# A decoder of four layers on one core: another PSUM bank and another order in the last steps of the self-attentions, and in the third cross-attention queries and rows through the bank of the outputs

## The reference

```python
def _layernorm(x, axis=-1, eps=1e-05):
    m = jnp.mean(x, axis=axis, keepdims=True)
    v = jnp.var(x, axis=axis, keepdims=True)
    return (x - m) / jnp.sqrt(v + eps)
...
    x = _layernorm(x + _L3_attn_ref(x, L3_attn_w_qkv, ...), axis=-1)
    x = _layernorm(x + _L3_xattn_ref(x, ctx_768, ...), axis=-1)
```

```python
        Qp = query @ Wq + bq
        K = _l2norm(key @ Wk + bk)
        V = value @ Wv + bv
        Q = _l2norm(Qp)
        ...
        out = out @ Wo + bo
        x = out + Qp
        ...
        return (x - mu) / jnp.sqrt(var + LN_EPS) * ln_gamma + ln_beta
```

## Time and profile before

| | before |
|---|---|
| median of 3 runs | 1782.21 us (1781.29 to 1782.80) |
| the profiled execution: its own time | 1781.73 us |
| span of its trace | 1779.9 us |
| PE busy, of the span | 1575.1 us, 88% |
| DVE, ACT, POOL busy | 51%, 38%, 23% |
| mean granted PE clock, of full speed | 0.949 |
| chain that ended last, PE / DVE / issue / POOL / DMA | 70% / 12% / 7% / 3% / 3% |

### The profile page before, as it was taken

How to read it: one execution, slowest core, us unless ns; L and a number is a source line. 1 busy time by engine, 2 the same in 40 slices (tenths; PEclk the granted TensorE clock), 3 DMA queues, 4 the chain that set the end, 5 groups by cost and what they waited for, 6 DMA issues and landing times.

```text
span 1779.9 us, 40044 instructions
## 1 busy us (share of the span) xinstructions
PE 1575.1 (88%) x14910; PEld 1296.3 (73%) x14910; DVE 908.8 (51%) x2316; ACT 680.0 (38%) x1611; POOL 411.6 (23%) x627
## 2 busy tenths in 40 slices
PE   7998998799986889998798688996996999999998
PEld 6875776588975657776688566775884776789897
DVE  3665887511106647777210472556344555565854
ACT  3334876222323337662122224551661444211110
POOL 2224776500004421112000243442121111000101
PEclk9999999989998989998899798997997999999999
DMA  5343000378851011101686101101001010033232
GB/s 203 147 150 133 28 26 20 114 267 294 320 197 38 1 53 30 43 15 50 255 302 217 52 1 45 40 27 48 1 1 60 28 38 5 25 105 108 79 111 68
DMA packets 41852, 166.76 MB, mean 94 GB/s; under 512 B 5984, under 2 KB 16864, under 8 KB 30176
## 3 DMA queue, kind: packets, MB, share of 16 engines
q1 hardware_dynamic: 39392, 159.14, 25.7%
q0 software_dynamic: 2304, 5.51, 1.0%
HBM read 140.22 MB, written 24.41 MB: 92 GB/s over the span
## 4 chain that ended last, share of the span: by engine, by line
PE 70%; DVE 12%; issue 7%; POOL 3%; DMA 3%; ACT 2%; SPq 1%; DVEq 0%; POOLq 0%; ACTq 0%
PE bank L1908 7%; PE bank L1921 6%; PE bank L1850 4%; PE bank L1852 4%; PE bank L1851 4%; PE bank L1330 4%; PE bank L1317 3%; PE bank L857 3%; PE bank L866 3%; PE bank L831 2%; DMA xrow<-slots 2%; PE bank L958 1%; PE bank L1344 1%; PE bank L1560 1%; PE bank L1305 1%
## 5 line engine op out<-in xcount | busy, mean ns | idle before, releaser
L3487 POOL TENSOR_TENSOR mv<-mv,cst 112x1 f32<-112x1 f32 x88 | 20.8, 237 | 602.0 <-DVE mv L2563 602.0
L2272 ACT ACTIVATE arena<-big,nm 112x375 f32<-112x375 f32 x256 | 144.0, 605 | 25.0 <-DVE nm L3174 16.3
L2482 ACT ACTIVATE htile<-bank,wup 128x128 f32<-128x128 f32 x280 | 80.1, 368 | 189.8 <-PE bank L1908 189.8
L1908 PE MATMUL bank<-xtile,wup 128*128 128x128 f32 x1120 | 135.1, 280 | 0.2
L1908 PEld LDWEIGHTS bank<-xtile,wup 128*128 128x128 f32 x1120 | 132.1, 197 | 1.1 <-DVE xtile L3334 1.0
L1330 PEld LDWEIGHTS bank<-cst,arena 112*125 112x125 f32 x768 | 98.3, 193 | 42.9 <-issue 19.5
L1921 PE MATMUL bank<-wdn,htile 128*128 128x256 f32 x560 | 126.3, 379 | 0.0
L3350 DVE COPY yrow<-bank 128x256 f32<-128x256 f32 x35 | 14.9, 425 | 217.6 <-PE bank L1921 217.6
L1330 PE MATMUL bank<-cst,arena 112*125 112x112 f32 x768 | 113.5, 286 | 7.7 <-POOL arena L3651 4.0
L1921 PEld LDWEIGHTS bank<-wdn,htile 128*128 128x128 f32 x560 | 103.9, 190 | 12.8
L3651 POOL TENSOR_SCALAR arena<-arena,c_lo 112x375 f32<-112x375 f32 x64 | 98.2, 1546 | 33.6 <-ACT c_lo L2276 33.5
(11 more groups left out here) (386 smaller groups left out, 3745.9 us busy)
## 6 DMA issues: line engine op xcount, KB each, us to landing
wup<-in_moe_up SPq DMA_DIRECT2D x35, 1028.0 KB, 7.3
wdn<-in_moe_dn SPq DMA_DIRECT2D x35, 1024.0 KB, 5.5
vspace<-in_ring SPq DMA_DIRECT2D x40, 512.0 KB, 4.3
ctxs<-parts SPq DMA_DIRECT2D x30, 564.0 KB, 3.8
slots<-mlpw SPq DMA_DIRECT2D x11, 1024.0 KB, 6.5
parts<-ctxs SPq DMA_DIRECT2D x8, 564.0 KB, 3.1
xrow<-slots SPq DMA_DIRECT2D x35, 128.0 KB, 5.1
slots<-yrow SPq DMA_DIRECT2D x35, 128.0 KB, 7.2
```

Source lines behind the costliest of these rows:

```text
L1908: mm = pe.matmul(bank[2 + 2 * (g % 2) + m // 4][:, m % 4 * ROWS:(m % 4 + 1) * ROWS], wup[:, g % 3, k * HID + 128 * m:k * HID + 128 * m + 1 ...
L2272: nc.scalar.activation(c_pr[:, g, j, :], c_sc[:, g % 2, j, :], ACT.Exp, bias=nm[:, p, h:h + 1], scale=-1.0).then_inc(cexp_done, 1)
L2482: ins = nc.scalar.activation(htile[:, g % 2, m, :], bank[2 + 2 * (g % 2) + m // 4][:, m % 4 * ROWS:(m % 4 + 1) * ROWS], func, bias=wup[:, ...
```

## The change

Six edits, on PE, DVE and ACT:

1. Drain of `causal`, `rope` and `linear`: steps 8 and 9 have a function of their own, `drain`. Batch 7's rows, columns and projection go through `bank[2]`, which held scores, and no longer wait for batch 6's residual or rows.
2. The drains have other `warm` products: three behind `output_rows`, one ahead of `project_rows`, three in step 9. `causal` and `rope` had two in step 8 and four in step 9, `linear` none.
3. On DVE `split_kv` moves from step 7 to step 9, between `stats(7)` and `rows_out(7)`.
4. In the drain of `rope` on DVE batch 6's `stats` and `rows_out` stand ahead of batch 7's `output_in`; in `causal` and `linear` its `stats` stand ahead of `output_normed(7)`.
5. Drain of `diff`, DVE: `stats(6)` ahead of `scaled(7)`.
6. `cross_normed`: `queries_t` and `rows_t` go through `OT`; `queries_t` waits for `cq_done` only, `project_rows(b-1)` comes ahead of `rows_t(b-2)` and no longer waits for `xt_done`, and `values(b-1)` now waits for `cq_done` and for `xt_done` of batch `b-3`.

```diff
-            def output_rows(sub, b):
+            def output_rows(sub, b, ps=TL):
                 pe.wait_ge(cot_in, at(sub, "t1", b, 1))
...
@@ causal, PE
+                def fillers(n):
+                    for _ in range(n):
+                        warm(bank[3], 256)
+
+                def drain(b, p, one):
+                    if one:
+                        output_rows(sub, b - 1, bank[2])
+                        fillers(3)
+                        output_columns(sub, b - 1, bank[2])
+                    else:
+                        fillers(3)
+                    rows_t(sub, b - 2, p, bank[5])
+                    if one:
+                        fillers(1)
+                        project_rows(sub, b - 1, bank[2])
+
                 def step(b, g, p, back, more, one, two):
+                    if not back[0]:
+                        drain(b, p, one)
+                        return
...
-                        for _ in range(0 if back[0] else 4 - 2 * one):
-                            warm(bank[4], 256)
...
@@ rope, PE
+                def drain(b, p, one):
+                    if one:
+                        values_turned(sub, b - 1, 1 - p)
+                    else:
+                        fillers(3)
+                    rows_t(sub, b - 2, p, bank[5])
+                    if one:
+                        output_rows(sub, b - 1, bank[2])
+                        fillers(3)
+                        output_columns(sub, b - 1, bank[2])
+                        fillers(1)
+                        project_rows(sub, b - 1, bank[2])
...
@@ cross_normed, PE
-                pe.wait_ge(ck_done, at(sub, "c2", 0, 1))
-                queries_t(0, 0, TL)
+                queries_t(0, 0, OT)
...
                         if one:
+                            pe.wait_ge(cq_done, at(sub, "c1", b if back[0] else B - 1, 1))
+                            if not isinstance(b, int) or b >= 3:
+                                pe.wait_ge(xt_done, xt_at(sub, b - 3))
                             values(b - 1, 1 - p)
...
                         if more:
-                            if one:
-                                pe.wait_ge(con_step, at(sub, "t2", b, 0))
-                            pe.wait_ge(cv_done, at(sub, "c3", b, 1))
-                            queries_t(b + 1, 1 - p, TL)
+                            pe.wait_ge(cq_done, at(sub, "c1", b, 1))
+                            queries_t(b + 1, 1 - p, OT)
...
+                        if one:
+                            project_rows(sub, b - 1)
                         if two:
-                            if one:
-                                pe.wait_ge(cob_done, at(sub, "t1", b - 1, 1))
-                            rows_t(sub, b - 2, p)
-                        if one:
-                            if two:
-                                pe.wait_ge(xt_done, xt_at(sub, b - 2))
-                            project_rows(sub, b - 1)
+                            if more:
+                                pe.wait_ge(cq_done, at(sub, "c1", b + 1, 1))
+                            rows_t(sub, b - 2, p, OT)
...
@@ diff, DVE
+                    if two and not back[0]:
+                        stats(sub, b - 2, p, 0)
                     if one:
                         scaled(b - 1)
                     if two:
-                        stats(sub, b - 2, p, 0)
+                        if back[0]:
+                            stats(sub, b - 2, p, 0)
                         rows_out(sub, b - 2, p)
...
@@ rope, DVE (causal and linear: without output_in, and output_normed ahead of rows_out)
+                def drain(b, p, one):
+                    residual(sub, b - 2, p, TL if one else bank[2])
+                    stats(sub, b - 2, p, 0)
+                    if not one:
+                        split_kv(SUBS[sub.index + 1])
+                    rows_out(sub, b - 2, p)
+                    if one:
+                        output_in(sub, b - 1, so_ready, at(sub, "o1", b, 0))
+                        output_normed(sub, b - 1, bank[2])
+                        output_columns(sub, b - 1, bank[2])
...
-                    if isinstance(b, int) and b == B - 1:
-                        split_kv(SUBS[sub.index + 1])
```

More of the change, by code:

```diff
@@ L1230, in linear, with fillers @@
                 wait_rows(pe, sub, B - 1)
+                def fillers(n):
+                    for _ in range(n):
+                        warm(bank[3], 256)
+                def drain(b, p, one):
+                    if one:
+                        output_rows(sub, b - 1, bank[2])
+                        fillers(3)
+                        output_columns(sub, b - 1, bank[2])
+                    else:
+                        fillers(3)
+                    rows_t(sub, b - 2, p)
+                    if one:
+                        fillers(1)
+                        project_rows(sub, b - 1, bank[2])
                 def step(b, g, p, back, more, one, two):
+                    if not back[0]:
+                        drain(b, p, one)
+                        return
                     if back[0]:
```

37 lines of the change are left out of this document (16 added, 21 removed).

## The result

| | before | changed |
|---|---|---|
| median, all executions on record | 1777.09 us (20 runs, 1769.87 to 1784.51) | 1768.91 us (20 runs, 1762.31 to 1777.97) |
| ratio | | 0.9944, 95% interval 0.9928 to 0.9961 |
| the profiled execution, and its span | 1781.73 us, 1779.9 us | 1772.88 us, 1771.1 us |

By the ratio the change saves 0.56%, 10.0 us (0.0056 of 1777.09; by the interval 6.9 to 12.8); the two medians lie 8.2 us apart. Two later timings gave 0.9940 and 0.9935. The forecast was 6 us. The three runs shown ahead of the prediction had a median of 1782.21 us, the twenty have 1777.09, so both kernels stand some 5 us lower than the forecast assumed.

The account below looks back on a forecast made before the run. PE bound the kernel (busy 88% of the span); only waits where its chain leaves PE could gain. Terms -0.5 `diff`, -0.4 `rope`, -0.5 `causal`, -4.4 `linear`, -2.9 third cross, +2.7 `split_kv` summed to -6.0: 1776 us, range 1771 to 1782.

Parts of the forecast that it names:

- Batch loop, 0: Third cross-attention, steps 0 to 5: PE reaches the keys sooner but waits for the context transfer; 0 us gained.
- Its end, -2.9: Third cross-attention, steps 6 to 8: no transfer left to wait for, projections start sooner; -2.9 us, bounds -2.4 and -3.0.
- steps 6 and 7: End of the third cross-attention: projection earlier in step 6, -1.0 us; `values(7)` earlier after step 7, -0.4 us.
- step 8: End of the third cross-attention: the projection starts at 1215.55 instead of waiting for rows and copy until 1217.08; -1.5 us.
- `linear`, -4.4: Drain of `linear`: batch 7's residual comes 4.4 us sooner at 2.4 GHz, which was assumed; -1.2 at 1.2 GHz.
- The third rival: Clock stays high in the drains and beyond, or the transfer does not bound the loop: -9 to -13 us, 1771; 14%.
- `causal`, -0.5: Drain of `causal`: +0.9 us at 1.2 GHz, -1.9 at 2.4 GHz soon after the transposes; the middle taken, -0.5.
- `rope`, -0.4: Drain of `rope`: batch 6's residual sooner; batch 7's +1.05 to -2.15 us by the clock, -0.4 taken for a halfway rise.
- `diff`, -0.5: Drain of `diff`: batch 6's `xln` ready before the `warm` product ends, so rows start sooner; -0.5 us, bounds 0 and -0.5.
- `split_kv`, +2.7: Step 9 of `rope`, `causal`, `linear`: `split_kv` holds up POOL's root; +0.9 us each, +2.7 in all, bounds +0.6 and +2.9.
- The rival of a slower kernel: Batch loop: PE's 1 us wait for the transfer lowers the clock; +3.6 us if in four steps, +17 in six; 4%.
- The rival that all `warm` products run at 1.2 GHz: Three drains: +0.9 us `causal`, +1.05 `rope`, -1.2 `linear`; +0.1 to +0.6 with the rest, 1782 us; 16%.

Follow-up runs that it names:

- e_cross: The kernel before with only the edits of `cross_normed`; median 1773.67 us against 1778.89 before, ratio 0.9977.
- e_split7: The changed kernel with `split_kv` put back to the end of step 7; median 1769.62 us, ratio 0.9945 against the kernel before.
- e_all: The changed kernel unaltered, run again; median 1769.67 us against 1778.89 before, ratio 0.9940.

## Why the prediction was right or wrong

The direction held, and each wait that was said to go went. The measured median, 1768.91 us, lies below the range of 1771 to 1782. Of the 7.1 us between it and the forecast of 1776, 5.1 are the starting point (1782.21 in three runs, 1777.09 in twenty), and 2 are the terms, which gave 6 us where the medians have 8.2 and the ratio 10.0. **The step that failed is the granted clock in and around the drains:** `causal` and `rope` were priced halfway between the two levels, and what the clock gives or takes outside the two residuals was put at nothing.

**Batch loop, 0: right.** From the first to the last issue of the context it is 77.83 us before and 77.27 after, 0.11 for each of five intervals. The reason given, the transfer, is shown by the pair with a third of the context. PE's wait moved from `xln` and `xT` to the transfer, as foretold.

**Its end, -2.9: right.** From the last issue to the residual of batch 7 it went from 43.71 (1175.45 to 1219.16) to 40.53 us (1176.70 to 1217.23), -3.2. To `values(7)` it is -1.7, where steps 6 and 7 were to give -1.4; from there to the residual -1.5, as said for step 8. With the 0.56 of the loop that is 3.7, the distance 0 to 7 of the table.

**`linear`, -4.4: right in the drain, too small around it.** 6 to 7 fell from 8.96 to 4.48 us, and was 4.47 to 4.49 in every trace with the new drain and its `warm` products. But 5 to next fell by 5.9 (71.91 to 66.05, means of the table), where -4.4 and +0.9 make -3.5. Some 0.9 of the other 2.4 lie ahead of the drain, from batch 5 to 6. At 2.4 GHz throughout that distance took 9.41 us in e_cross and e_split7 and 8.78 in e_all, because the residual of batch 6 stood behind `split_kv` here too (in e_split7 `split_kv` ran from 1330.93 for 1.21 us, the residual came at 1332.06): 0.6 us that the prediction counted for `rope` alone. The rest is the clock, most of it behind batch 7, where the distance fell by 0.4 us though `split_kv` cost 0.89. In the first trace the kernel before was at 0.51 from 1344 to 1357 us, part of the drain and the first keys of the fourth cross-attention included, and the changed one at 0.57 for less than 4 us there. Windows, before and then changed:

```profile
1344.00:1357.00 13.00, 8.66 (x30) 6.92 (x29) 2.96 (x10) 1.56 (x4) 1.14 (x3) 0.51 0.29 92
```

```profile
1344.30:1348.00 3.70, 3.55 (x14) 3.55 (x15) 0.37 (x3) 0.92 (x2) 0.40 (x1) 0.57 0.51 134
1349.00:1356.00 7.00, 5.16 (x40) 2.83 (x38) 3.57 (x4) 1.20 (x4) 2.83 (x5) 1.00 0.43 169
```

The third rival ("the clock stays high in the drains and beyond"), given 14%, is what happened here; its other half, that the transfer is not the bound, did not.

**`causal`, -0.5: wrong.** "I take the middle" was the failing step. The clock was at 2.4 GHz from the columns on in the ten traces that had the new drain with its `warm` products, and 6 to 7 fell by 2.2 us against the first trace. A part of those 2.2 was the first trace's own: two other executions with the old drain had 5.75 there, not 6.68. From 5 to next, `split_kv` and the clock behind included, 1.4 us are left in the means (57.44 to 56.08), where -0.5 and +0.9 make +0.4.

**`rope`, -0.4: the sum came out, but by luck.** The term was for the residual of batch 7, with that of batch 6 coming sooner. Up to there (in the table 5 to next less 7 to next) the means of three and four traces went from 20.2 to 17.7 us, -2.5 where -0.4 was expected, and the four differ by 2.8 with the clock. Behind it the distance grew by 2.0, where +0.9 was expected. The two misses cancel: 5 to next went from 66.25 to 65.80, -0.45, where -0.4 and +0.9 make +0.5.

**`diff`, -0.5: mis-sized, and the clock around it took more than it gave.** From the start of the last `warm` products ahead of the rows to the residual of batch 7 it is 3.80 us before (144.55 to 148.35) and 3.01 after (145.62 to 148.63), so -0.8; 6 to 7 in all fell by 1.0. But 5 to next grew by 2.6 (72.37 to 74.93, means). Ahead of the edit, 5 to 6 took 1.3 to 1.7 us longer in the four traces, and the windows show the clock there at 0.80 where it was 0.89. e_split7, which has the edit of `diff` too, stood at 0.89 and took 15.70. Windows, before, changed and e_split7:

```profile
123.68:139.36 15.68, 13.46 (x151) 10.20 (x150) 11.12 (x28) 5.58 (x11) 4.10 (x6) 0.89 0.38 153
```

```profile
123.37:140.69 17.32, 15.10 (x151) 11.72 (x150) 11.12 (x29) 5.92 (x11) 4.10 (x6) 0.80 0.38 155
```

```profile
123.65:139.35 15.70, 13.48 (x151) 10.19 (x150) 11.11 (x29) 5.72 (x11) 4.10 (x6) 0.89 0.38 153
```

Whether the edits make that more likely, or the draws fell so, is not settled.

**`split_kv`, +2.7: right for the collision.** 1.08 us for POOL's first root instruction, 3.14 for 2.25 us to `xln`, +0.89 in each of three drains. With the clock behind it, it cost more (2.0 us in `rope`), and undoing it gave the faster kernel.

Summed over the table, the terms are +2.6, -0.45, -1.4, -5.9 and -3.7 (`diff`, `rope`, `causal`, `linear`, third cross), -8.8, where the medians of the twenty runs give -8.2 and their ratio -10.0; the forecast had -0.5, +0.5, +0.4, -3.5, -2.9. `linear` and `causal` gained more than forecast, `diff` lost. The rival of a slower kernel, the clock falling in the loop for want of work, did not show in the distances from batch 1 to 5 (15.3 to 15.9 us in the first trace). The rival that all `warm` products run at 1.2 GHz fell for `causal` and `linear`.

## What to carry to other kernels

Ahead of a reorder ask which transfer is issued behind the work that is to come sooner: here about 1 us a batch lay hidden under a transfer, and came out only when two thirds of it were left out or issued earlier. A wait on one engine is a free place for an instruction only if that instruction does not slow the engine that is waited for: the same 1.2 us of DVE work cost 0.89 us beside POOL's root and nothing there 2.4 to 2.7 us earlier, beside PE's projection. Price a removed wait with the clock behind it too, over several executions, since one trace shows one draw of it.

## What the runs showed that was not expected

- One program's executions differ by 15 us on one core. The distances that repeat do so to 0.01 us; where they don't, in the places looked at, it is where stretches of 1.2 GHz fall. The stage from the residual of batch 7 in the third cross-attention to the first of `linear`, with the same instructions, took 59.7 us in the kernel before and 54.4 in e_cross. Windows of that place, the changed kernel (59.78 us) and then e_cross (54.42):

```profile
1217.20:1247.00 29.80, 22.48 (x92) 17.69 (x91) 19.12 (x57) 4.38 (x14) 8.39 (x21) 0.69 0.19 71
```

```profile
1216.80:1241.20 24.40, 18.79 (x91) 15.15 (x91) 19.10 (x57) 4.37 (x14) 7.92 (x21) 0.86 0.23 87
```

- Beside a DVE instruction with two SBUF inputs POOL's instruction on 112 x 1 elements does not merely run slower by some factor. It ended just behind the DVE instruction: 0.06 us behind `split_kv` (1343.22 against 1343.16), having taken 1.08 us, and 0.04 us behind a shorter one, having taken 0.56. The Trainium skill calls this an exclusive lock (SBUF — State Buffer, "Who interferes with whom"); the trace agrees.
- The keys started without a wait 2.84 us after the issue of a transfer of 126 columns (504 bytes a row, 384 rows, 189 KB); behind one of 1504 bytes a row (564 KB) they started after 3.60 us in the changed kernel and 3.79 us before, and waited for it both times.
